# A convolution sequence in fp32 on one core: y times t1 moved behind the single taps, its bank changed, weights loaded once

## What is computed

```python
t1 = p1_w * x
t2 = x + t1
t4 = relu(x)
t5 = unfold(x, 3, 7, padding 1, 3)              # n, c, 21, h, w
t7 = einsum('oc,nchw->nohw', p7_w, t4)
t8 = unfold(t7, 1, 5, dilation 3, padding 6)
t9 = x[:, :, None] - t8
t10 = einsum('ngihw,goi->ngohw', t2 in 4 groups, p10_w)   # n, c*21, h, w
t11 = einsum('nck,nmk->ncm', t1, t5) / sqrt(h*w)
t12 = t9.mean(2)
t13 = einsum('ncm,nmk->nck', t11, t10) / sqrt(c*21)
out = maximum(t13, t12)
```

## Time and profile before

| what | us |
|---|---|
| median of 3 runs | 396.9 (396.81 to 397.4) |
| the profiled execution, its time | 396.71 |
| its span, first to last instruction | 394.9 |
| PE busy | 384.3 (97%) |
| DVE busy | 328.7 (83%) |
| ACT busy | 249.4 (63%) |
| POOL busy | 85.2 (22%) |
| PE share of the chain that ended last | 88% |

### The profile page before, as it was taken

One profiled execution on the slowest core, in us unless ns is written; L12 is line 12 of the kernel. 1 busy time (PEld: TensorE's weight loads), 2 busy tenths in 40 slices (PEclk: granted clock), 3 DMA queues, 4 the chain that ended last, 5 costly groups with the idle time before them and its releaser, 6 DMA issues.

```text
span 394.9 us, 10235 instructions
## 1 busy us (share of the span) xinstructions
PE 384.3 (97%) x4034; PEld 170.0 (43%) x4034; DVE 328.7 (83%) x397; ACT 249.4 (63%) x713; POOL 85.2 (22%) x72
## 2 busy tenths in 40 slices
PE   5999899999999999999999999999999999999996
PEld 2222274433733338333463336533383333733383
DVE  5988996999989886888968889688878889688645
ACT  1044548677767682776736775667726768377790
POOL 0443003322022220222122220222202222122300
PEclk9999999999999999999999999999999999999999
DMA  8999409675777937768577855769377793463115
GB/s 313 407 409 408 180 11 375 223 239 210 228 256 255 328 125 241 271 242 275 169 240 251 266 187 201 227 252 334 114 251 236 261 315 113 140 208 110 54 56 212
DMA packets 28848, 90.75 MB, mean 230 GB/s; under 512 B 3328, under 2 KB 3840, under 8 KB 28800
## 3 DMA queue, kind: packets, MB, share of 16 engines
q1 hardware_dynamic: 28800, 90.09, 65.4%
HBM read 73.30 MB, written 16.78 MB: 228 GB/s over the span
## 4 chain that ended last, share of the span: by engine, by line
PE 88%; DVE 6%; DMA 2%; issue 1%; SPq 1%; ACT 0%; DVEq 0%; ACTq 0%
PE ps_y L756 39%; PE ps_y L841 15%; PE ps_t L778 12%; PE ps_p L778 11%; PE ps_y L767 8%; DMA xw<-x_conv 2%; PE ps_y L994 1%; PE ps_y L778 1%; DVE yT L555 1%; DVE box L582 1%; DVE v_planes L516 1%; DVE v_planes L510 1%; DVE pair_sum L565 1%; DVE t1T L588 1%; DVE ps_y L542 0%
## 5 line engine op out<-in xcount | busy, mean ns | idle before, releaser
L756 PE MATMUL ps_y<-v_planes,u_planes 64*64 64x512 f32 x1536 | 191.9, 595 | 2.7 <-DVE v_planes L516 1.8
L255 POOL TENSOR_TENSOR t1T<-t1T,p1T_sb 128x512 f32<-128x512 f32 x60 | 77.5, 1314 | 273.8 <-PE ps_y L767 230.2
L348 ACT ACTIVATE t<-xn,p_plus 128x64 f32<-128x64 f32 x512 | 128.0, 334 | 0.0
L778 PE MATMUL ps_p<-box,p_fifth 64*64 64x512 f32 x440 | 113.1, 589 | 1.8 <-DVE box L582 1.8
L778 PE MATMUL ps_t<-t,aT 64*64 64x512 f32 x440 | 113.2, 590 | 0.2
L756 PEld LDWEIGHTS ps_y<-v_planes,u_planes 64*64 64x64 f32 x1536 | 57.3, 132 | 118.7 <-issue 103.3
L555 DVE STREAM_TRANSPOSE yT<-ps_y 128x512 f32<-128x512 f32 x64 | 42.0, 695 | 36.5 <-PE ps_y L767 36.5
L286 ACT ACTIVATE base<-ps_p 128x512 f32<-128x512 f32 x57 | 34.0, 597 | 59.4 <-PE ps_p L778 58.6
L841 PEld LDWEIGHTS ps_y<-t1T,yT 128*128 128x128 f32 x512 | 57.8, 192 | 6.5 <-issue 6.5
L841 PE MATMUL ps_y<-t1T,yT 128*128 128x128 f32 x512 | 59.3, 277 | 0.0
L596 DVE TENSOR_TENSOR base<-ps_t,base 128x512 f32<-128x512 f32 x56 | 38.4, 686 | 11.7 <-PE ps_t L778 11.5
(11 more groups left out here) (57 smaller groups left out, 148.3 us busy)
## 6 DMA issues: line engine op xcount, KB each, us to landing
xw<-x_conv SPq DMA_DIRECT2D x64, 561.0 KB, 6.6
xn<-x_nat SPq DMA_DIRECT2D x32, 512.0 KB, 4.4
t1T<-x_pix SPq DMA_DIRECT2D x32, 512.0 KB, 5.3
out<-base SPq DMA_DIRECT2D x63, 256.0 KB, 4.8
u_planes<-w_tiles SPq DMA_DIRECT2D x4, 672.0 KB, 8.8
out<-base SPq DMA_DIRECT2D x2, 128.0 KB, 2.0
p1T_sb<-p1T SPq DMA_DIRECT2D x1, 128.0 KB, 11.0
p_sb<-p7T SPq DMA_DIRECT2D x1, 64.0 KB, 10.8
```

The lines of the kernel that those rows point to most:

```text
L255: nc.gpsimd.tensor_tensor(part, part, p1T_sb[:, e, :].unsqueeze(1).broadcast_to([P, 4, C]), ALU.mult).then_inc(t1_ready, 1)
L348: last = nc.scalar.activation(t2[:, h, W * r:W * (r + 1)], xn[:, f, at:at + W], ACT.Copy, scale=p1_plus[:, 8 * h + r:8 * h + r + 1])
L756: last = nc.tensor.matmul(dst[TILE * pair:TILE * pair + TILE, :], weights_of(rows_of(half), u, weights, TILE * k, TILE), data_of(rows_of(h ...
L778: last = nc.tensor.matmul(dst[cols, 0:data.shape[-1]], weights[rows, cols], data[rows, :], start=start, stop=False, skip_group_check=True)
```

## The change

Five things are changed.

- TensorE: `y_times_t1` stands behind `single_taps` in slots 5, 9, 13, ... It writes to `ps_t13`, the bank of the t13 products, in all images but the last, and waits for the last maximum of the image before it (`out_ready, 8 * n`). The wait of `one_two` for `aT_ready` is gone.
- ScalarE: `scale_a` comes behind the copy of that slot and behind both t2 halves 6 and 7; in the last image the seed of half 1 comes ahead of base 0.
- VectorE: in the steady loop `box_fours` and `box_last` of quarter 3, and all of quarter 0 of the next image, come behind the turn and the seeds of the following slot; the maximum of half 7 comes right behind `box_pairs`. In image 0 the first two box operations of quarter 1 take the place of the two `t1_quarter`, which GpSimd does now, as it does all eight parts, three behind each of m_done 2 and 3 and two behind m_done 4.
- Weights: w_tiles holds each group once (336 KB). `weights` makes the combinations in three dependent additions, and new copies on ScalarE (`swap`, two of 64 partitions and 448 columns a group) write the exchanged halves for planes 1 and 3.
- Loads: the back half of the first unit's x comes in two pieces (9 and 8 of 17 blocks), and its plane 1 is made in two pieces.

```diff
                 outputs_second(p_b, t_b, item_b)
+                single_taps(u)
                 if turned is not None:
                     y_times_t1(turned)
-                single_taps(u)
...
             pair_second(0, 2)
+            single_taps(5)
             y_times_t1(0)
             p7_whole(0, 4)
-            single_taps(5)
...
         def a_bank(n):
-            return ps_y[(GROUPS * (n + 1) + 2) % SETS][0]
+            return ps_t13 if n < LAST else ps_y[(GROUPS * N_IMG + 2) % SETS][0]
...
             def y_times_t1(n):
                 pe.wait_ge(y_turned, 8 * n + 8)
                 pe.wait_ge(t1_ready, 8 * n + 8)
+                if n == 0:
+                    pe.wait_ge(base_ready, 2)
+                elif n < LAST:
+                    pe.wait_ge(out_ready, 8 * n)
...
                     wait(pe, y_turned, 2 * (u - SETS) + 2)
-                    if u % GROUPS == 2:
-                        wait(pe, aT_ready, u // GROUPS)
...
+            def swap(g):
+                if g < 2:
+                    act.wait_ge(u_steps, U_STEPS * (g + 1))
+                else:
+                    act.wait_ge(u_later, U_STEPS * (g - 1))
+                for half in range(2):
+                    copy(u_planes[TILE * half:TILE * half + TILE, g, U_3:U_1 + 1, :],
+                         u_planes[TILE - TILE * half:P - TILE * half, g, OUTER:U_1_FRONT + 1, :]).then_inc(u_swapped, 1)
...
+            swap(0)
+            swap(1)
             copy_two(0)
+            swap(2)
             copy_two(1)
...
             relu(0, 0)
+            swap(3)
...
-            for q in range(4):
-                pool.wait_ge(m_done, 2 + q // 2)
+            for q in range(8):
+                pool.wait_ge(m_done, 2 + q // 3)
                 t1_part(0, q)
...
+                    for blocks, loaded in ((slice(0, FIRST_BLOCKS), xw_part),
+                                           (slice(FIRST_BLOCKS, BLOCKS_IN), xw_loaded[0][BACK])):
+                        dve.wait_ge(loaded, 16)
+                        nc.vector.tensor_tensor(inner(0, V_1)[:, blocks], x1[:, blocks], x2[:, blocks],
+                                                ALU.add).then_inc(early_ready, 1)
...
-                base_half(n, 0)
-                seed_x(n, 1)
+                if n < LAST:
+                    base_half(n, 0)
+                    seed_x(n, 1)
+            seed_x(LAST, 1)
+            base_half(LAST, 0)
```

More of the change, by code:

```diff
@@ L19 @@
 BLOCKS_IN = 17
+FIRST_BLOCKS = 9
 PAIRS = 32
@@ L41 @@
 FRONT, BACK = range(2)
-U_0, U_2, U_1, U_3 = (FRONT, 0), (FRONT, 1), (BACK, 1), (BACK, 2)
+U_0, U_2, OUTER, U_1_FRONT, U_3, U_1 = range(6)
 V_0, V_2, V_1, V_3 = range(4)
@@ L174, in load_group @@
                 for order in range(2):
-                    sp.dma_start(xw[:, u % 3, order], x_conv[u // GROUPS, u % GROUPS, order]).then_inc(
-                        xw_loaded[u % 3][order], 16)
+                    first = 0
+                    if u == 0 and order == BACK:
+                        first = FIRST_BLOCKS
+                        sp.dma_start(xw[:, 0, BACK, :, 0:first], x_conv[0, 0, BACK, :, :, 0:first]).then_inc(xw_part, 16)
+                    sp.dma_start(xw[:, u % 3, order, :, first:], x_conv[u // GROUPS, u % GROUPS, order, :, :, first:]
+                                 ).then_inc(xw_loaded[u % 3][order], 16)
             def load_natural(n, f):
@@ L475, in weights @@
                 dve.wait_ge(w_loaded[g], 16)
[L476 to L477 removed]
+                u = u_planes[:, g]
+                nc.vector.tensor_tensor(u[:, U_1], u[:, U_0], u[:, OUTER], ALU.add).then_inc(u_steps, 1)
                 dve.wait_ge(u_steps, U_STEPS * g + 1)
[L479 to L480 removed]
+                nc.vector.tensor_tensor(u[:, U_1_FRONT], u[:, U_1], u[:, U_2], ALU.add).then_inc(u_steps, 1)
+                dve.wait_ge(u_steps, U_STEPS * g + 2)
+                nc.vector.tensor_tensor(u[:, U_2], u[:, U_1], u[:, U_2], ALU.subtract).then_inc(u_steps, 1)
             def first_rows(b, order):
@@ L699, in _ @@
                 seeds(u + 1)
-                box_last(n, 0)
+                box_fours(n - 1, 3)
+                box_last(n - 1, 3)
+                box_sums(n, 0)
                 max_half(n - 1, 0)
@@ L744, in weights_of @@
             def weights_of(rows, u, plane, at, width):
-                order, row = plane
-                return u_planes[rows, u % GROUPS, order, row, at:at + width]
+                return u_planes[rows, u % GROUPS, plane, at:at + width]
             def data_of(rows, u, plane, block):
@@ L1009, in weight_tiles @@
     w = p10.reshape(GROUPS, CG, KH, KW, CG)
-    out = np.zeros((GROUPS, P, 2, KH, WCOLS), p10.dtype)
+    out = np.zeros((GROUPS, P, KH, WCOLS), p10.dtype)
     for g in range(GROUPS):
-        for order in range(2):
-            for quarter, phase in enumerate(PHASES_OF[g % 2, order]):
-                rows = slice(CG * quarter, CG * quarter + CG)
-                for k, (pair, at) in enumerate(DENSE[phase <= 2]):
-                    for s in range(2):
-                        tap = phase + PHASES * (at - 1) - (2 * pair + s)
-                        out[g, rows, order, :, TILE * k + CG * s:TILE * k + CG * s + CG] = w[g, :, :, tap]
-                to, at = SINGLE[phase]
-                out[g, rows, order, :, 3 * TILE:] = w[g, :, :, phase + PHASES * (at - 1) - to]
+        for quarter, phase in enumerate(PHASES_OF[g % 2, FRONT]):
+            rows = slice(CG * quarter, CG * quarter + CG)
+            for k, (pair, at) in enumerate(DENSE[phase <= 2]):
+                for s in range(2):
+                    tap = phase + PHASES * (at - 1) - (2 * pair + s)
+                    out[g, rows, :, TILE * k + CG * s:TILE * k + CG * s + CG] = w[g, :, :, tap]
+            to, at = SINGLE[phase]
+            out[g, rows, :, 3 * TILE:] = w[g, :, :, phase + PHASES * (at - 1) - to]
     return out
```

59 lines of the change are left out of this document (25 added, 34 removed).

## The result

The changed kernel takes **433.2 us** (median of 6 runs, 427.40 to 433.71) against 397.1 us before (6 runs of the same series, 396.65 to 397.40): a ratio of 1.0887, 95% interval 1.0831 to 1.0943. It is slower by 36 us, where 395.0 us and a range of 393.2 to 396.7 us were forecast. The profiled execution took 432.65 us with a span of 430.9 us.

A forecast was written before the change was run, and what follows sets the result against it. TensorE's own work bounds the whole images, so only time before 83 us and after 362 us can be won. The steps' gains and losses sum to -1.85 us, taking 396.9 to 395.0 us (range 393.2 to 396.7).

The forecast's parts named there:

- Step 5: y times t1 moved, images 1 to 6: loss 0.2 us, plus 0.35 once; box operations moved behind turn and seeds free.
- Rival C: Head of y times t1, each image: TensorE waits for a late maximum holding the bank; 399.7 us, chance 0.06.
- Step 1: Start: halved weight loads and split first plane bring first products sooner, 7.85 and 12.1 us; gain 1.05 us (0.7 to 1.4).
- Step 2: Unit 4's slot: box operations replace quarters, TensorE's wait for box 1 goes; gain 1.9 us, loss 0.15.
- Step 3: Behind units 1 and 2: GpSimd's third t1 part meets a VectorE box operation; loss 1.05 us (0 to 1.3).
- rival A: GpSimd's third part costs nothing and the loads gain in full: 393.6 us, chance 0.2.
- Step 4: First y times t1: p7 waits for its seed, loss 0.6 us; VectorE gets 7.3 us, slot 7 gains 1.15.
- Rival D: Slot 7's wait was really for image 1's loads, so its 1.15 us stay: 396.2 us, chance 0.07.
- Step 6: End, last image: seed of half 1 written ahead of base 0; gain 0.1 us (0 to 0.7).

The follow-up runs named there:

- the kernel with the relu behind: Changed kernel with ScalarE's second relu of each image moved behind base of half 5 and the seed of half 6: 430.36 us, ratio 1.0850.
- the start alone: Kernel before with only the weights loaded once and completed by ScalarE, and the first load in two pieces: 396.05 us against 396.70, ratio 0.9987.
- the two mended waits: Two yT buffers and GpSimd quarters two at a time, plus three edits for two small TensorE waits at the beginning: 394.52 us, ratio 0.9949.
- the last kernel: The kernel of the two mended waits with two VectorE maxima done sooner, ahead of box operations: 393.42 us against 396.63, ratio 0.9917.

## Why the prediction was wrong, point by point

**Step 5 failed, in the sentence on the box operations that are moved behind the turn and the seeds.** It said that they fill VectorE's gap there at no cost. I took the turn to be released by the single taps, as in the other slots, and never asked what else it waits for. I also passed over that before, in the slot with y times t1, it came only at 157.10 us, behind y times t1. In the trace of before the wait for a_done could not be seen, since m_done came later; it stands in `turn_y` in plain sight. The price: VectorE shut out 7.84 us an image, with 40 us of work in 46.7, so that the seed of half 6 and the maximum of half 0 are late for TensorE. An image goes from 46.77 us (148.53 to 195.30 in the kernel with two buffers, between two y times t1) to 52.49 us (155.01 to 207.50). Of these 5.72 us the two waits are 2.87. The work from the t13 rows to the single taps takes 4.31 us (172.54 to 176.85) in place of the 2.73 it takes at full clock (170.84 to 173.57 in the kernel with the relu behind): 1.58 us for the clock. The rest, 1.27 us, I put down mostly to work that ran side by side and now doesn't (p7 rows alone, 1.08 us, then t13 rows with dense calls). This part is argued and not isolated; an image that kept its clock in the kernel with the relu behind has 1.02 us of it (50.81 less 46.77 less a wait of 3.02). Two more images of the series take 53.4 us.

**Rival C named the right sign, with the wrong place, the wrong mechanism and too small a price.** It had TensorE wait at the head of y times t1 for the maximum of half 7 and the bank of A, and priced that by one GpSimd meeting an image. In the six images no such wait repeats: the one row of it is the 0.42 us of slot 9. TensorE waits in the slot behind, for the seed of half 6 and the maximum of half 0, because of a wait of VectorE's that I had not looked at, and the price was 6 us an image, not 0.45 or 0.8. The period's growth by more than 0.15 us was the sign named for it, and is how the trace gives it away.

What else step 5 said holds in the kernel with two yT buffers. From one y times t1 to the next it is 46.77 us and was 46.73 (148.40 to 195.13), so the changed transitions cost 0.04 x 6 = 0.24 us; 0.2 were forecast. The maximum of half 7 and the scaled A cost TensorE nothing. Slot 9's once-only wait was 0.42 us for 0.35:

```profile
101.68 7.38 PE L871 MATMUL ps_t<-t1T,yT 128*128 128x128 f32 x64 [0.42 <-DVE base L626]
```

**Step 1, the start: right in kind, over-sized.** In the changed kernel:

```profile
8.00 3.12 PE L785 MATMUL ps_y<-v_planes,u_planes 64*64 64x512 f32 x24 [1.54 <-DVE v_planes L532]
```

8.00 and not 7.85, and the second unit at 12.23 for 12.1. But over the profiled executions of the kernels with this start the first product came between 7.74 and 8.64 us, with the landing of x, so the one row of before, 8.74, gives 0.1 to 1.0 us and not 0.7 to 1.4.

**Step 2: the wait of 1.79 us for box 1 is gone**, as said. **Step 3: right.** The two laid-out meetings both happened, also the one in unit 1's slot, for which there was room as said (with GpSimd two at a time VectorE idles 1.02 us ahead of the next turn, with three not at all):

```profile
29.50 2.32 DVE L610 TENSOR_TENSOR box<-pair_sum 128x1024 f32<-128x1024 f32 x1
```

Each costs 2.33 - 1.22 = 1.11 us (1.07 taken from the row at 68.44), and taking the third part away gave 1.1 us, so my 1.05 stands and rival A falls. The Trainium skill's rule (SBUF — State Buffer, "SBUF: two separate sides": a VectorE operation with two SBUF inputs and a GpSimd one that reads SBUF shut each other out for a whole instruction) would make it a whole part, by estimate 3.75 / 3 = 1.25 us here; 1.11 us was measured, 0.14 us less, so the trace agrees nearly. The lateness showed as two TensorE waits of 0.29 and 0.44 us and in the two slots as a whole.

**Step 4: both amounts near, both a little large, one reason wrong.** p7 of half 5 waited 0.47 us for its seed (0.6 forecast), and slot 7 went from 11.04 us (70.94 to 81.98) to 10.16 in the kernel with two yT buffers (70.25 to 80.41), 0.88 us of the 1.15; in the changed kernel it is 10.23. But VectorE did not get the 7.3 us of y times t1 for the turn and the seeds, as this step says: in the changed kernel the same unseen wait held unit 4's turn until 59.77 us, behind y times t1 (52.26 to 59.6), 2.7 us sooner than before (62.46) and not 7. That slot 7 gained nearly the forecast amount with this reason wrong is luck. The maxima in that slot are so close that each microsecond won ahead of them partly returns as a wait: the start alone and the two mended waits both showed it. Rival D is out, since the maxima moved in the last kernel took slot 7 to 9.96 us. **Step 6: right**; from the last full single taps to the last it takes 7.83 us (361.57 to 369.40) and took 7.97 (362.32 to 370.29).

**The sum without the failed step.** The kernel with two yT buffers is the change as I had understood it: 1.14 us faster than before by medians (1.2 by the ratio), where I had 1.85. The missing 0.7 us are the start (0.4 to 0.5) and slot 7 (0.27); the other terms are off by little, and in both directions. That would have been 395.7 by my 396.9, within the range; the range as given left no room for a wait that I had not read.

## What to carry to other kernels

Before an instruction is moved across another on an engine's list, read every wait of the one that is now first, in the code and not in the trace: a wait that is always met early leaves no row, and it is the one that bites when the order changes. A single buffer that is read as a whole ties the start of the next round to the end of the last; what the writing engine can do meanwhile has to stand ahead of it. And for an engine in order, add its busy time and the time it is shut out: 40.0 + 7.8 against 46.7 us says that no re-sorting behind the turn can bring the old period back. The two orders tried here did not come near even the 47.8; whether another does is open.

## What was not expected of the hardware

A stall of TensorE can cost twice its length, and not always. In the kernel with the relu moved behind, TensorE waits about the same in each image, yet the images differ. Busy time of two images in a row, then the stretch behind the wait in each:

```profile
153.40:204.21 50.81, 47.79 (x517) 21.18 (x513) 39.95 (x48) 31.19 (x90) 10.04 (x8) 1.00 0.64 215
204.21:257.72 53.51, 50.65 (x516) 22.77 (x512) 39.96 (x48) 31.25 (x90) 10.04 (x8) 0.94 0.60 206
...
170.84:176.00 5.16, 5.16 (x67) 1.97 (x71) 5.16 (x7) 2.21 (x6) 1.03 (x1) 1.00 0.45 182
221.49:228.00 6.51, 6.51 (x52) 1.94 (x52) 4.25 (x5) 0.97 (x2) 0.00 (x0) 0.54 0.48 190
```

The waits ahead of them:

```profile
170.84 0.65 PE L807 MATMUL ps_t<-t,aT 64*64 64x512 f32 x2 [3.02 <-DVE base L626]
...
221.49 1.12 PE L807 MATMUL ps_t<-t,aT 64*64 64x512 f32 x2 [2.86 <-DVE base L626]
```

After 3.02 us the granted clock stayed at 1.00 (2.4 GHz) and the image took 50.81 us; after 2.86 us it was 0.54, which is 1.2 GHz for most of the stretch, and the image took 53.51: 2.7 us more for the same work and the same VectorE time. Against the 46.77 us of the kernel with two buffers the first stall cost 4.0 us and the second 6.7. Before its wait TensorE had been busy without a pause in both. Of five images in that trace one kept the full clock. The runs of the changed kernel differ in the same way: five at a mean granted clock of 0.963 or 0.964 took 432.65 to 433.71 us, and one at 0.976 took 427.40. What decides between the two these runs do not settle; a forecast of a stall of this length has to carry both prices.
